# Third expert layer: results written run by run and gathered batch by batch, with the first eight steps of two attentions in batch order

## What is computed

```python
# attention 2 (attention 3 is alike, without gamma, bias and gate)
xn = _layernorm(x, ln_gamma, ln_beta)
q = (xn @ w_q).reshape(B, SQ, NUM_HEADS, DIM_HEAD)          # 16 heads of 64
scores = jnp.einsum('bqhd,bkhd->bhqk', q * SCALE, k)
attn = jax.nn.softmax(scores, axis=-1)
out = jnp.einsum('bhqk,bkhd->bqhd', attn, v).reshape(B, SQ, INNER)
out = out @ w_out + b_out

# expert layer 2: 8 experts of 128 -> 256 -> 128, the best two for each token
top_vals, top_idx = jax.lax.top_k(gate_logits, TOP_K)
h = jax.nn.gelu(jnp.einsum('td,edf->etf', xt, w1), approximate=False)
y = jnp.einsum('etf,efd->etd', h, w2)
out = jnp.einsum('te,etd->td', combine, y)
```

## Times and profile before

| what | us |
|---|---|
| median of three executions | 1168.32 (1166.42 to 1173.46) |
| profiled execution, its span | 1219.8 |
| attention 2, first maxima (L2278) | 530.86 |
| expert layer 2, first to last `weigh` (L2030) | 791.1 to 848.7 |
| attention 3, first maxima | 875.33 |

### The profile page before, as it was taken

How to read it: one execution, slowest core, us unless ns; L and a number is a source line. 1 busy time by engine, 2 the same in 40 slices (tenths; PEclk the granted TensorE clock), 3 DMA queues, 4 the chain that set the end, 5 groups by cost and what they waited for, 6 DMA issues and landing times.

```text
span 1219.8 us, 22199 instructions
## 1 busy us (share of the span) xinstructions
PE 1054.1 (86%) x6815; PEld 797.4 (65%) x6815; DVE 717.3 (59%) x2444; ACT 643.9 (53%) x2117; POOL 571.5 (47%) x926
## 2 busy tenths in 40 slices
PE   4988999758889998979999987777799999977994
PEld 3865788735555667856767665566566776654994
DVE  5575354476776771386767784322876776852444
ACT  2244323357778723358778862222387888731321
POOL 5223655451000152566555656366375555655452
PEclk9987999989999988889999997697899999986997
DMA  2003556599600124110000001364300000014665
GB/s 63 13 27 112 161 165 208 163 156 385 237 1 1 36 68 137 54 30 19 1 19 19 1 5 43 85 187 121 87 19 1 2 1 1 2 33 129 200 208 173
DMA packets 116005, 102.87 MB, mean 84 GB/s; under 512 B 18027, under 2 KB 97571, under 8 KB 115888
## 3 DMA queue, kind: packets, MB, share of 16 engines
q1 hardware_dynamic: 105280, 82.71, 23.3%
q0 software_dynamic: 8448, 17.20, 4.2%
q10 hardware_dynamic: 2160, 1.53, 0.5%
HBM read 65.04 MB, written 36.36 MB: 83 GB/s over the span
## 4 chain that ended last, share of the span: by engine, by line
PE 61%; DVE 16%; issue 6%; ACT 5%; POOL 4%; DMA 4%; another core or an unknown queue 3%; SPq 2%; DVEq 0%; ACTq 0%; POOLq 0%
PE ps L2973 4%; PE ps L2777 4%; PE ps L2869 4%; PE ps L2882 4%; PE ps L2779 4%; PE ps L2778 4%; PE ps L2987 3%; PE ps L3515 3%; PE ps L3519 3%; PE ps L3168 2%; PE ps L3528 2%; PE ps L3001 2%; PE ps L3327 2%; ACT ex L1323 2%
## 5 line engine op out<-in xcount | busy, mean ns | idle before, releaser
L1323 ACT ACTIVATE ex<-ps,nmx 128x154 f32<-128x154 f32 x512 | 194.0, 391 | 75.0 <-DVE nmx L2278 73.2
L1085 POOL TENSOR_TENSOR pp<-ex,rc 128x256 f32<-128x256 f32 x256 | 157.6, 615 | 146.0 <-DVE rc L2283 145.0
L2278 DVE TENSOR_REDUCE nmx<-ps 128x2 f32<-128x308 f32 x256 | 119.6, 470 | 60.2 <-PE ps L2779 59.2
L922 POOL DMA_INDIRECT yq_d<-yq,ids_q x78 | 74.7, 957 | 79.4 <-DVE yq L2030 60.6
L2973 PEld LDWEIGHTS ps<-ident,pp 128*128 128x128 f32 x640 | 73.9, 142 | 55.5 <-POOL pp L1086 46.5
L2777 PE MATMUL ps<-kp,q_s 128*128 128x308 f32 x256 | 95.5, 373 | 15.1 <-ACT ex L1323 12.6
L1323 ACT ACTIVATION_READ_ACCUMULATOR ex<-ps,nmx 128x1 f32 x512 | 105.2, 205 | 0.0
L2973 PE MATMUL ps<-ident,pp 128*128 128x128 f32 x640 | 100.1, 280 | 2.8 <-POOL pp L1086 2.8
L1440 ACT ACTIVATE pe<-ps,nmx 128x154 f32<-128x154 f32 x256 | 84.9, 394 | 32.0 <-DVE nmx L2161 30.9
L892 POOL TENSOR_TENSOR ln_r<-ln_v,mhalf 128x4 f32<-128x4 f32 x32 | 32.7, 1021 | 105.4 <-DVE ln_v L1736 86.8
L2869 PE MATMUL ps<-xc_q,w_q 128*128 128x256 f32 (+1 forms) x276 | 63.6, 371 | 19.3 <-issue 11.5
(11 more groups left out here) (481 smaller groups left out, 2831.6 us busy)
## 6 DMA issues: line engine op xcount, KB each, us to landing
w_r<-in_L_ffn_W SPq DMA_DIRECT2D x69, 256.0 KB
xq_d<-blankq SPq DMA_DIRECT2D x4, 4160.0 KB, 23.8
w_q<-in_L_ffn_W SPq DMA_DIRECT2D x46, 256.0 KB
w_q<-in_L_ffn_w SPq DMA_DIRECT2D x46, 128.0 KB
xq<-xq_d SPq DMA_DIRECT2D x24, 130.0 KB
w_s<-in_L_ffn_W SPq DMA_DIRECT2D x8, 256.0 KB
w_e<-in_L_ffn_W SPq DMA_DIRECT2D x8, 256.0 KB, 5.2
acc<-yq_d SPq DMA_DIRECT2D x8, 256.0 KB, 4.6
```

Of the source, the lines that this page charges most:

```text
L922: pool.indirect_dma_start(yq_d[:, :], bass.IndirectOffsetOnAxis(ap=ids_q[:, c:c + 1], axis=0), yq[k % NY][:, h, :], None).then_inc(q_out[k ...
L1085: pool.tensor_tensor(pp[st % 2][:, m % 4, 2 * j:2 * j + 2, :], w[:, :, 0:P], r.broadcast_to([P, 2, P]), ALU.mult)
L1323: ins = act.activation(ex[:, tt % NEX, j, :], ps[:, tt % 3, j * SK:(j + 1) * SK], ACT.Exp, bias=nmx8[:, tt % 8, j:j + 1], accum_out=sm8[:, ...
L2278: dve.tensor_reduce(nmx8[:, tt % 8, :], ps[:, tt % 3, 0:2 * SK].rearrange("p (h s) -> p h s", h=2), AX.X, ALU.max, negate=True).then_inc(n ...
```

## The change

Four things are done together.

1. **Results of the third expert layer.** For l = 2 POOL's 39 scatters, DVE's `targets` and SP's eight loads are gone. SP writes `yq` of each run to a new table `yl_d`, in the order in which the runs lie (`results(k)`, one DMA a run, after the weights of a later run). In attention 3 POOL fetches them back by `slot_q`, with 32 indirect DMAs of 128 rows (`fetch(b, i)`, eight a batch): 12 ahead of the first `rstd`, 6 more ahead of the first tile, and 14 in steps 0 to 3 at the places in `FETCH_AT`. DVE makes the row numbers for SP with two more small instructions.
2. **Blank rows.** `yl_d` is filled once from `blankq`, by two more DMAs on SP beside those that fill `xq_d`, early in the kernel.
3. **Order of steps.** The first eight steps go batch by batch: both groups 0 and 1 of batch 0, then of batch 1, and so on. So x of batch b is first needed in step 2b. Its sum, statistics and `rstd` are moved into steps 0, 2, 4 and its normalisation, `turned_x` and `low_x` into steps 1, 3, 5. This holds for both attentions 2 and 3.
4. **Preparation.** `PREP_AT` replaces `SPOT`: group 2 in steps 2, 3, 4, 7, 8 and group 3 in steps 5 and 7 to 12. `PRIOR` is 12 for l = 3, and ahead of `normed(0)` there are 12 where there were 10.

```diff
-    PRIOR = (None, None, 7, 8)
-    SPOT = (0, 2, 3, 4, 5, 6, 7, 8, 9, 10, 11, 12, 13)
+    PRIOR = (None, None, 7, 12)
+    PREP_AT = {(2, 0): [(2, 0)], (2, 2): [(2, 1)], (3, 0): [(2, 4)], (3, 1): [(2, 5)], (3, 3): [(2, 6)], (4, 0): [(2, 7)], (5, 0): [(3, 0)],
+               (7, 0): [(2, 8), (2, 9)], (7, 1): [(2, 10)], (7, 2): [(2, 11)], (7, 3): [(3, 1)],
+               (8, 0): [(2, 2)], (8, 1): [(2, 3)], (8, 2): [(2, 12)], (8, 3): [(3, 4)], (9, 0): [(3, 5)], (9, 1): [(3, 6)], (9, 3): [(3, 7)],
+               (10, 0): [(3, 2)], (10, 1): [(3, 3)], (10, 2): [(3, 12)], (11, 0): [(3, 8)], (11, 1): [(3, 9)], (12, 0): [(3, 10)], (12, 1): [(3, 11)]}
-    ORDER = [(g, b) for g in range(2) for b in range(B)] + [(2, 0), (2, 1), (3, 0), (3, 1), (2, 2), (3, 2), (2, 3), (3, 3)]
+    ORDER = [(g, b) for b in range(B) for g in range(2)] + [(2, 0), (2, 1), (3, 0), (3, 1), (2, 2), (3, 2), (2, 3), (3, 3)]
-    BEHIND = {(0, "A"): [("x", 1)], (0, "C"): [("x", 2)], (2, "A"): [("x", 3)], (13, "A"): [("f", 0)], (14, "A"): [("f", 1)], (14, "D"): [("t", 0)], (15, "A"): [("lg", 0)], (15, "D"): [("t", 1)]}
+    FETCH_AT = {(0, 1): (2, 2), (0, 3): (2, 3), (0, 5): (2, 4), (0, 6): (2, 5), (1, 1): (2, 6), (1, 3): (2, 7), (1, 5): (3, 0), (2, 1): (3, 1), (2, 3): (3, 2),
+                (2, 5): (3, 3), (2, 6): (3, 4), (3, 1): (3, 5), (3, 3): (3, 6), (3, 5): (3, 7)}
+    BEHIND = {(1, "A"): [("x", 1)], (3, "A"): [("x", 2)], (5, "A"): [("x", 3)], (13, "A"): [("f", 0)], (14, "A"): [("f", 1)], (14, "D"): [("t", 0)], (15, "A"): [("lg", 0)], (15, "D"): [("t", 1)]}
## The prediction, made region, SP
+                def results(k):
+
+                    sp.wait_ge(q_y, max(run(l, k), 1))
+                    r = sp.value_load(row_y[0:1, UNIT[k]:UNIT[k] + 1])
+                    sp.wait_ge(q_y, run(l, k) + 1)
+                    sp.dma_start(yl_d[bass.ds(r, P * TALL[k]), :].rearrange("(p h) c -> p h c", h=TALL[k]), yq[k % NY][:, 0:TALL[k], :]).then_inc(q_lin[k % NY], 16)
...
+                    if l == 2:
+                        results(k - NQ)
+                if l == 2:
+                    for k in range(NRUN - NQ, NRUN):
+                        results(k)
+                    return
## The prediction, made blank rows, SP
+                for h in range(2):
+                    sp.dma_start(yl_d[h * EMPTY // 2:(h + 1) * EMPTY // 2, :].rearrange("(k p) c -> p k c", p=P),
+                                 blankq[:, 0:1, 0:D].broadcast_to([P, EMPTY // (2 * P), D])).then_inc(q_init, 16)
## The prediction, made region, POOL
-                for k in range(NRUN):
+                for k in range(NRUN if l == 3 else 0):
## The prediction, made attention, POOL
+                def fetch(b, i):
+
+                    c, n = i % 2, i // 2
+                    into = (acc, y_other)[c]
+                    pool.indirect_dma_start(into[:, b * S + n * D:b * S + (n + 1) * D], None, yl_d[0:EMPTY, :],
+                                            bass.IndirectOffsetOnAxis(ap=slot_q[:, b, c * TB + n:c * TB + n + 1], axis=0)).then_inc(y_row[b], 16)
...
                     for m in range(8):
                         normalise(st, m)
...
+                        if l == 3 and (st, m) in FETCH_AT:
+                            fetch(*FETCH_AT[st, m])
+                        if st in (0, 2, 4) and m == 7:
+                            rstd(2 * l, st // 2 + 1)
+                        elif st in (1, 3, 5) and m == 4:
+                            low_x((st + 1) // 2)
## The prediction, made attention, DVE
+                    begins, ends = st // 2 + 1 if st in (0, 2, 4) else None, (st + 1) // 2 if st in (1, 3, 5) else None
                     maxima(st, 0)
                     low_out(st - 2, 0)
                     copy_pt(st - 1, 1)
+                    if ends:
+                        normed_half(ends, 0)
                     maxima(st, 1)
                     step_prep(st, 0)
+                    if ends:
+                        normed_half(ends, 1)
+                    elif begins and l == 3:
+                        second_added(5, begins)
...
                     maxima(st, 7)
                     step_prep(st, 3)
+                    if begins:
+                        variances(begins)
## The prediction, made attention, PE
                     scores(st, 1)
                     step_prep(st, 1)
-                    if st == 0:
-                        turned_x(1)
-                    elif st == 2:
-                        turned_x(3)
+                    if st in (1, 3, 5):
+                        turned_x((st + 1) // 2)
```

More of the change, by code:

```diff
@@ L93, in spot @@
             def spot(k):
-                return [("prep", st // B + 1, SPOT.index(4 * (st % B) + k))] if B <= st < NST - B and 4 * (st % B) + k in SPOT else []
+                return [("prep", g, i) for g, i in PREP_AT.get((st, k), [])]
             def behind(at):
@@ L503, in xattn_moe_stack @@
         ln_shift = z_bm
+        q_lin, lin_from = s_wr + k_w[4:6] + [in_x], [48 * ((NRUN + NW - 1 - u) // NW) for u in range(NW)] + [32, 32, 16 * B]
+        row_y = ids_q[:, 0:NRUN]
+        y_row, row_from = [k_out, k_s[0], k_s[1], in_ctx], [16 * NT, 16 * 3 * E // 2, 16 * 3 * E // 2, 16]
         c_hi_ok = sem("c_hi_ok"); c_ok = sem("c_ok")
@@ L1131, in normalise_heads @@
                     return
+                if l == 3:
+                    for k in range(NRUN - NY, NRUN):
+                        pool.wait_ge(*sent(2, k))
+                    for i in range(2 * TB):
+                        fetch(0, i)
+                    for i in range(4):
+                        fetch(1, i)
                 rstd(2 * l, 0)
-                rstd(2 * l, 1)
+                if l == 3:
+                    fetch(1, 4)
+                    fetch(1, 5)
                 low_x(0)
-                rstd(2 * l, 2)
+                if l == 3:
+                    fetch(1, 6)
+                    fetch(1, 7)
+                    fetch(2, 0)
+                    fetch(2, 1)
                 for st in range(NST):
@@ L1311, in step_prep @@
                 def step_prep(st, k):
-                    if B <= st < NST - B and 4 * (st % B) + k in SPOT:
-                        prep(l, st // B + 1, SPOT.index(4 * (st % B) + k))
+                    for g, i in PREP_AT.get((st, k), []):
+                        prep(l, g, i)
                 def exps(st, m):
@@ L1377, in heads @@
                     step_prep(st, 2)
-                    if st == 0:
-                        turned_x(2)
                     exps(st, 6)
@@ L1766, in layer_norm, with second_added @@
                     between(B)
+            def second_added(s, b):
+                dve.wait_ge(*((y_row[b], row_from[b] + 16 * 2 * TB) if s == 5 else (y_in[b], 80)))
+                link(dve.tensor_tensor(x_tok[:, tiles(b), :], x_tok[:, tiles(b), :], y_other[:, bsl(b)].rearrange("p (n d) -> p n d", n=TB), ALU.add))
             def finish(s, b):
@@ L1776, in finish @@
                 else:
-                    dve.wait_ge(y_in[b], 80 if s == 5 else 112)
-                    link(dve.tensor_tensor(x_tok[:, tiles(b), :], x_tok[:, tiles(b), :], y_other[:, bsl(b)].rearrange("p (n d) -> p n d", n=TB), ALU.add))
+                    if s == 7:
+                        second_added(s, b)
                     more = acc[:, bsl(b)]
```

80 lines of the change are left out of this document (32 added, 48 removed).

## The result

The changed kernel took **1205.46 us** (median of four, 1202.58 to 1209.78) against 1170.12 us for the kernel before on the same chip (1166.42 to 1173.46): a ratio of **1.030**, 95% interval 1.0265 to 1.0334. It is slower, as forecast, but by 35 us where 13 were forecast, and outside the range.

What follows compares the result with a forecast made beforehand. POOL's scatters were taken to bound much of the third expert layer, PE the attentions. Terms -10 - 1 + 9 + 14 = +12 on 1168.3 gave 1180, and 1181 us with row numbers; own range 1173 to 1189, overall 1153 to 1194.

Steps and rivals of the forecast that it cites:

- The expert layer without scatters: Third expert layer: removing POOL's scatters and small targets, adding writes on SP, gains 10 us (-15.5 to 0).
- PE's idle time is truly at stake: Third expert layer: at PE's free pace the tiles take 39 us instead of 58; idle time 15.5 us.
- the prediction's own test: Third expert layer in the trace after: first to last weigh should take about 48 us, 58 before.
- From the last result to attention 3's first maxima: Stretch between third expert layer and attention 3: 24.6 us where it was 26.2, -1 us (-3 to +2).
- The bubble in steps 1, 3 and 5: Attentions 2 and 3: PE waits at turned_x for late normalisation, 4.2 us, 3.6 in step 3 (2.2 to 5).
- Attention 2: Start -2, step 0 -1, PE's waits at turned_x 12, other steps unchanged in total: +9 us (+2 to +12).
- Attention 3: Steps 0 to 5: POOL's fetches and PE's waits add +5, +4.7 and +4.2: +14 us (+5 to +18).
- The blank rows: Two more writes on SP early in the kernel, costing nothing: 0 (-0 to +2).
- The rule against the fetches: Fetches meeting DVE's sums in steps 0 and 2 would add 1 to 4 us to attention 3; left out of the sum.
- PE has room in the first steps: Rival, chance 0.18: a hold at turned_x overlaps with a round trip, costing about 0.5 us each; 1153 us.
- the expert layer's gain eats the bubbles: Rival, chance 0.24: expert layer gains 15.5 us and waits at turned_x cost 3 instead of 4.2; 1167 us.
- POOL bounding the attention and SP the expert layer: Rival, chance 0.16: fetches take 2 us, adding 10 in steps 0 to 3, or SP's writes cancel the gain; 1191 us.

Runs made afterwards that it cites:

- e5: The changed kernel with the linear writes of the third expert layer's results issued by POOL instead of SP: 1201.82 us, ratio 1.0269.
- e2: The changed kernel with the third expert layer's results scattered by POOL and loaded by SP as before, order of steps as after: 1193.98 us, ratio 1.0248.
- e4: The changed kernel with normalisation of batches 1 to 3 moved forward and results scattered as before: 1168.55 us, ratio 0.9992.
- e1: The changed kernel with sum, statistics, rstd and normalisation of batches 1 to 3 moved some five tiles forward: 1186.5 us, ratio 1.0165.
- e3: The changed kernel with 14 unused products ahead of PE's wait for normalised x in steps 1, 3 and 5: 1193.28 us, ratio 1.0242.

## Why the prediction was right or wrong

**"The expert layer without scatters", -10 us: wrong in sign, +5.4.** The step that failed is "PE's idle time is truly at stake". The 15.5 us of idle time, the 15.1 us of waiting for scatters and the 58 us were read from an execution that had been disturbed just there, by 14 us in this stage alone; 11.0 of the 15.5 us had no cause in the profile, and "remote" could not be read as the landing of scatters. This term alone is 15.4 us of the 22.6 by which the loss came out larger than forecast. The prediction noted that its trace was 4.4% long, took this for an even scaling and went on. The lower end of its range, that SP's queue gives back what is won, named the right mechanism (a write between the weights of two runs) but stopped at nothing won; e5 shows that it cost 5.5 us. That the stage measured 49.0 us, near the "about 48" of the prediction's own test, is chance: it is a loss on 43.6, not a gain on 58.

**"From the last result to attention 3's first maxima", -1 us: +0.5, within its range.** A fetch took about 0.97 us and 0.16 to 0.30 of issuing, where 1.26 in all was taken. e2, with scatters, is at 23.5 us, so the gather costs 3.6 here and the shorter start wins 3.1 (between e4 and e1 the gather costs 1.2).

**"The bubble in steps 1, 3 and 5", 4.2 us: the mechanism, its place and the wait were right (4.57, and 4.5 on average over six), its price was not.** The prediction equated the wait with the loss. Two things differ: with the clock kept, a hold of 4.6 us lengthens step 1 by 2.8 only, so that PE had some 1.8 us of room after all; and the wait took PE's clock for the 5.8 us after it, 2.7 more. Sum 5.5. In step 3 of attention 2, where preparations fill some of the wait, 3.03 us are left of it, and the step takes 16.8 us where e1, with the same preparations and without the wait, takes 12.8.

**Attention 2, +9 us (to +12): +13.4** (15.1 less 1.7 at the start). The term that was mis-sized is the bubble, for the reason above: e3 takes 6.8 us off this attention by keeping the clock. The start gained as forecast. "The total of which is as before", for the other steps, is not borne out either: e4, whose longest wait at `turned_x` is 1.7 us, is still 4.7 over the attention of before, and why is open.

**Attention 3, +14 us (to +18): +19.9.** The term that was mis-sized is again the bubble with its clock, in steps 3 and 5: steps 2 to 5 came out at +13.0 where 8.9 were forecast, and e3 takes 4.5 off them. In steps 0 and 1 the sum was nearly right (29.0 us for 27.5), but not its way: step 0 took 9.4 and not 12.5. POOL's 12.3 us in step 1 are not "hidden in 10.8 + 4.2 = 15": they are not beside the bubble but ahead of it, since `rstd` stands in the same queue behind late tiles and fetches, and so the wait grew to 7.1 us and the step to 19.5. Scattering instead (e2) takes 7.4 us off attention 3, moving the normalisation (e1) 9.7, both (e4) 18.2: two causes that nearly add up.

**The blank rows, 0:** no run tells them alone. The four changed kernels without them reach the first maxima of attention 2 at 514.5, 514.9, 518.5 and 521.5 us, those with them between 516.6 and 523.9; nothing beyond that spread.

**The rule against the fetches.** The Trainium skill, SBUF — State Buffer, section "SBUF: two separate sides", gives about 3.1 us, against 0.62 alone, for a DMA of POOL's queue that meets a copy by DVE; both figures are the DMA's. The 32 fetches of the changed kernel took 0.94 to 1.07 us:

```profile
L1105 POOL DMA_INDIRECT acc<-yl_d,slot_q x16: 944/988/1067, 826.5 to 906.5; - x16
L1105 POOL DMA_INDIRECT y_other<-yl_d,slot_q x16: 941/955/1026, 827.8 to 910.6; - x16
```

Those among the tiles took 0.98 to 1.03 us, a few hundredths more than a scatter. Two that ran beside DVE's sums took 0.94 and 1.02, and the longest, 1.07, ran beside the normalisation of batch 0; these three landed 2.6 us after their start, which is the median of all. Nothing like the rule's price shows here.

**The rivals.** That PE has room in the first steps held for 1.8 us of a wait, not for all of it. That the expert layer's gain eats the bubbles fell with that gain. The third, POOL bounding the attention and SP the expert layer, is what happened on top of the forecast, with both halves at once, but not by its mechanism: it had been given 0.16 and a price of 10 us for fetches of 2 us each. The fetches took 0.97 and cost 8.5 us in attention 3 all the same, by their number in POOL's queue, and the writes cost 5.4 in the expert layer.

## What to carry to other kernels

Where the profiled execution is longer than the others by more than their spread, find the stage that holds the difference, by a second profile if need be, before a gain is counted there; here the whole gain was that difference, and waits without a cause in the profile were its sign. A wait put on the engine that bounds a stage has two prices, what it can't win back and what its clock loses afterwards; in step 1 of attention 2 the second was as large as the first. A queue that looks idle in busy time (SP, 0.36 us a write) can still be the bound by the time of its round per item, and work moved to an engine with slack must be counted with all that stands behind it in that engine's order.

## What the runs showed that was not expected

Of the hardware: PE's clock went to half in a single wait of 4.6 us and stayed there for the first 5.8 us of uninterrupted work behind it. Fourteen unneeded products in each of six waits took 11.3 us off the two attentions. And the expert layers took 14 us longer in one execution of the same program than in another while the attentions agreed to a tenth of a microsecond; what disturbed that execution was not found, only that its trace shows over 75 us of waits for "remote" and the other thirteen none.
